# Maxima, denominators and relative positions share one PSUM ring, scores get a fourth bank, and the FFN weights are rounded during attention

## What is computed

```python
q = q / sqrt(hd)
score = einsum('bhqd,bhkd->bhqk', q, k) + einsum('bhqd,qkd->bhqk', q, pe_k)      # pe = rel_emb[clip(k - q, -64, 64) + 64]
attn = softmax(score)
ctx = einsum('bhqk,bhkd->bhqd', attn, v) + einsum('bhqk,qkd->bhqd', attn, pe_v)
x = x + (ctx @ W_out + b_out)                 # on layernorm(x)
h = silu(xq @ wq_gate.T) * (xq @ wq_up.T)     # q: fp4_quant_dequant, blocks of 16
x = x + hq @ wq_down.T                        # on layernorm(x)
```

## Time and profile before

| | |
|---|---|
| three runs | 2486.07, 2490.33 and 2491.36 us, median 2490.33 |
| the profiled execution | 2487.88 us |
| its span, first to last instruction | 2486.2 us |
| mean granted TensorE clock | 0.972 |
| busy: PE, DVE, ACT, POOL | 95%, 77%, 58%, 24% of the span |
| projections and the start of attention | 0 to 173 us |
| attention's iterations | 173 to 2041 us |
| FFN weights | 2044 to 2091 us |
| FFN over 32 tiles | 2091 to 2486 us |

### The profile page before, as it was taken

The page is one execution under the profiler, slowest core; times in us unless marked ns, Lnnn a source line. Parts: engine busy times, 40 slices in busy tenths (PEclk is TensorE's granted clock), DMA queues, the critical chain, the costliest instruction groups (busy, mean ns, idle before and its releaser), DMA issues. The chain is left out here.

```text
span 2486.2 us, 48992 instructions
## 1 busy us (share of the span) xinstructions
PE 2349.4 (95%) x19372; PEld 1168.7 (47%) x19372; DVE 1910.8 (77%) x3509; ACT 1432.6 (58%) x2724; POOL 607.1 (24%) x361
## 2 busy tenths in 40 slices
PE   7899999999999999999999999999999974899997
PEld 3424444444444444444444444444444433666665
DVE  6687777777777777777777777777777707999997
ACT  3416666666666666666666666666666651434432
POOL 5402233222222222222223322222222220111111
PEclk9959999999999999999999999999999995999999
DMA  5733323332334333333323332333332211111110
GB/s 156 200 82 87 88 84 88 88 88 85 109 96 106 95 89 88 89 87 94 89 80 93 88 88 80 92 106 100 95 94 84 74 34 41 41 42 51 42 44 26
DMA packets 275666, 210.43 MB, mean 85 GB/s; under 512 B 17058, under 2 KB 266628, under 8 KB 275332
## 3 DMA queue, kind: packets, MB, share of 16 engines
q1 hardware_dynamic: 274308, 203.37, 30.0%
q0 software_dynamic: 1152, 4.19, 0.6%
HBM read 113.35 MB, written 93.34 MB: 83 GB/s over the span
## 5 line engine op out<-in xcount | busy, mean ns | idle before, releaser
L1049 DVE TENSOR_REDUCE amax<-psA 128x1 f32<-128x512 f32 x2048 | 1312.8, 684 | 407.0 <-PE psA L758 395.4
L1019 ACT ACTIVATE probs<-psS 128x512 f32<-128x512 f32 x1792 | 927.9, 609 | 411.2 <-PE psS L868 411.2
L758 PE MATMUL psA<-keys,queries 96*128 96x512 bf16 x2048 | 771.9, 390 | 1.6 <-DVE amax L1049 1.6
L868 PE MATMUL psS<-queries,keys 102*128 102x512 bf16 (+7 forms) x2176 | 637.5, 344 | 18.9 <-ACT probs L1019 4.1
L784 PE MATMUL psC<-probs,vals 128*32 128x512 f32 (+7 forms) x4352 | 475.0, 524 | 0.1
L719 POOL TENSOR_TENSOR band_probs<-band_probs,side 128x2048 f32<-128x2048 f32 x64 | 288.7, 4533 | 514.2 <-PE psC L880 514.2
L868 PEld LDWEIGHTS psS<-queries,keys 102*128 102x128 bf16 (+1 forms) x2176 | 195.8, 98 | 355.1 <-ACT probs L1019 157.4
L758 PEld LDWEIGHTS psA<-keys,queries 96*128 96x128 bf16 x2048 | 195.7, 97 | 345.5 <-DVE amax L1049 269.1
L1014 ACT ACTIVATE band_probs<-psS 128x512 f32<-128x512 f32 x256 | 153.0, 598 | 152.5 <-PE psS L857 152.3
L998 ACT COPY rel_scores<-psS 128x512 f32<-128x512 f32 x256 | 137.2, 590 | 72.8 <-PE psS L772 72.8
L784 PEld LDWEIGHTS psC<-probs,vals 128*32 128x32 f32 (+1 forms) x4352 | 89.1, 102 | 167.4 <-issue 86.1
(11 more groups left out here) (162 smaller groups left out, 2056.9 us busy)
## 6 DMA issues: line engine op xcount, KB each, us to landing
rel_skew<-rel_scores SPq DMA_DIRECT2D x32, 2048.0 KB, 7.6
rel_near<-rel_skew SPq DMA_DIRECT2D x64, 1024.0 KB, 8.2
keys<-k_ring SPq DMA_DIRECT2D x48, 256.0 KB, 5.8
queries<-q_parts SPq DMA_DIRECT2D x192, 64.0 KB, 2.4
ctx_d<-rden SPq DMA_DIRECT2D x32, 256.0 KB, 2.3
ctx_in<-ctx_d SPq DMA_DIRECT2D x32, 256.0 KB, 2.7
q_parts<-parts SPq DMA_DIRECT2D x16, 384.0 KB, 3.0
k_ring<-parts SPq DMA_DIRECT2D x12, 384.0 KB, 3.3
```

Of the source, the lines that this page charges most:

```text
L758: t.matmul(psA[:, (first + n) % ABANKS, :], qs[0:NR, qb, h, u * P:(u + 1) * P], keys[0:NR, par, h, c0:c0 + NQ], start=True, stop=True).the ...
L868: ins = t.matmul(bank[:, o:o + k], keys[0:nr, par, h, c0:c0 + P], qs[0:nr, qb, h, q0:q0 + k], start=True, stop=True, skip_group_check=True)
L1019: ins = a.activation(probs[:, n % 4, half], src, ACT.Exp)
L1049: v.reduce_max(amax[:, pair, k:k + 1], psA[:, (first + n) % ABANKS, :], AX.X).then_inc(max_taken, 1)
```

## The change

- psM goes. psS gets a fourth bank. P, D and B take slots in the psA ring of three, in TensorE's order (`SLOT`, counted out by `small_slots`); a product waits until the slot three places back was taken, whatever it held. T takes a slot of the psS ring.
- Each P has a slot and a mask of its own, four masks of 256 instead of two of 512. In `ORDER`, P moves ahead of the last M of its step and F ahead of M in step 12.
- The denominators are found by four transposes of `ctxs`, and VectorE reads one column per head. `c.sel` and its two GpSimd instructions go.
- The FFN weights and the bias columns are loaded during iteration 1, and rounded in place by VectorE during attention from iteration 2 on: 16 pieces of 256 or 352 columns, ten operations each, one operation at the start of each of steps 7 to 12. In `ffn_weights`, the transposes of the gate and up rows wait for nothing, VectorE copies out half of them, and W_out's bias products come last.

```diff
-    "SMSSMSMVMP", "SMSSMSMVMP", "SMSSMSMVFMP", "SMSSMSMVMP",
-    "SMSSMSVMF", "SMSSMSVMT", "SMSSMSVM", "SMSSMSVM",
+    "SMSSMSMVPM", "SMSSMSMVPM", "SMSSMSMVFPM", "SMSSMSMVPM",
+    "SMSSMSVFM", "SMSSMSVMT", "SMSSMSVM", "SMSSMSVM",
-SBANKS, ABANKS = 3, 3
+WSTEPS = range(7, 13)
+SBANKS, ABANKS = 4, 3
+def half_at(it, pl, half):
+    return 2 * (first_of(it) + pl) + half + it + 1 + (1 if it < LAST and pl >= place(2 * ASTEPS + 2) else 0)
+def small_slots():
+    slots = {}
+    def add(*key):
+        slots[key] = len(slots)
+    for n in range(ROUND):
+        add("M", 0, n)
+    for n in range(AHEAD):
+        add("M", 1, n)
+    for it in range(LAST + 1):
+        todo = [(it + 1, n) for n in range(AHEAD, ROUND)] if it < LAST else []
+        for step in range(STEPS):
+            if step == ASTEPS and it < LAST - 1:
+                todo.extend((it + 2, n) for n in range(AHEAD))
+            for kind in ORDER[step]:
+                if kind == "M" and todo:
+                    add("M", *todo.pop(0))
+                elif kind == "P":
+                    add("P", it, step - PSTEP)
+                elif kind in "DB" and it:
+                    add(kind, it - 1)
...
-        psM = ctx.enter_context(nc.psum_tensor("psM", [P, NQ], F32))
...
+            def slot_free(*key):
+                pe.wait_ge(small_taken, SLOT[key] + 1)
...
-                pe.wait_ge(max_taken, first + n + 1)
+                slot_free("M", m, n)
...
                 pe.wait_ge(negm_ready, m + 1)
-                t.transpose(psM[0:2 * APAIRS, 0:P], ...
+                pe.wait_ge(unit_done, turn_half(m) + 1)
+                t.transpose(psS[0:2 * APAIRS, turn_half(m) % SBANKS, 0:P], ...
...
                 pe.wait_ge(ctx_copied, it + 2)
+                slot_free("D", it)
                 for u in range(CH):
-                    ins = t.matmul(psM[:, HG * u:HG * u + HG], ctxs[:, u * P:(u + 1) * P], c.sel[:, 0:P:32],
-                                   start=True, stop=True, skip_group_check=True)
+                    ins = t.transpose(small("D", it)[:, u * P:(u + 1) * P], ctxs[:, u * P:(u + 1) * P], c.ident[:])
...
+                if it == 1:
+                    sp.wait_ge(w_set, 4)
+                    fw.load(nc, sp)
...
                 for step in range(STEPS):
+                    if step in WSTEPS and it > 1:
+                        next(weights, None)
...
+                    for kind in ORDER[step]:
+                        if kind == "M":
+                            if todo:
+                                take(*todo.pop(0))
+                            k += 1
+                            if RSTEP < step <= RSTEP + RUNITS and k == 3 and not ends:
+                                rel_maxima(it + 1, step - RSTEP - 1)
+                        elif kind == "P":
+                            mask_positions(step - PSTEP)
+                        elif kind == "D" and not first:
+                            invert(it - 1)
+                        elif kind == "B" and not first:
                             normalise(it - 1)
...
+            def weight_ops():
+                ch = Chain(dve, w_dve)
+                for i, f in [(i, f) for i in range(2) for f in range(FT)] + [(2, f) for f in range(4)]:
...
+                    if ch.n:
+                        ch.hold()
+                    ch.mark(v.tensor_reduce(scale, blk(x), AX.X, ALU.max, apply_absolute_value=True))
+                    yield
...
+                    ch.mark(v.tensor_mul(blk(x), blk(tmp), wide(scale)))
+                    yield
```

In `ffn_weights` after the change:

```diff
+            sp.wait_ge(o_zero, 1)
+            for h in range(HG):
+                sp.dma_start(wo[32 * h:32 * h + HD], w_out.rearrange("(g h d) n -> h d g n", g=NG, h=HG)[h]).then_inc(o_in, 16)
...
+            dve.wait_ge(fw.ends_in, 16 * 2 * HG)
+            oc.mark(v.tensor_scalar(fw.bvc[:], fw.bvc[:], fw.rvc[:, 0:1], None, ALU.add))
...
+            for k in range(KD):
+                dve.wait_ge(w_T, KD + k + 1)
+                v.tensor_copy(wgu[:, k, FFN:FFN + NQ], psW[1][:, k, 0, :]).then_inc(w_copied, 1)
+                v.tensor_copy(wgu[:, k, FFN + NQ:2 * FFN], psW[1][:, k, 1, 0:FFN - NQ]).then_inc(w_copied, 1)
...
             for i in range(2):
                 for k in range(KD):
                     for f in range(FT):
+                        ins = nc.tensor.transpose(psW[i][:, k, f // 4, (f % 4) * P:(f % 4 + 1) * P], fw.raw[i][:, f, k * P:(k + 1) * P],
                                                   c.ident[:])
+            pe.wait_ge(w_copied, 3 * KD)
```

More of the change, by code:

```diff
@@ L73 @@
 BF = 1.5 * 2.0 ** 22
+FT = -(-FFN // P)
+FLAST = FFN - (FT - 1) * P
+GU = FFN // 2
+TINY = 1e-12
 def semaphores(nc, ctx, names):
@@ L835, in half_free @@
                 def half_free(n, half):
-                    pe.wait_ge(unit_done, 2 * (base + place(n, ends)) + half + 1)
+                    pe.wait_ge(unit_done, half_at(it, place(n, ends), half) + 1)
                 def near_half(n, half):
@@ L842, in near_half @@
                     h = 2 * c2 + half
-                    bank = psS[:, (2 * (base + place(n, ends)) + half) % SBANKS, :]
+                    bank = psS[:, half_at(it, place(n, ends), half) % SBANKS, :]
                     if n == 0 and half == 0:
@@ L1009, in iteration @@
                     for half in range(2):
-                        act.wait_ge(unit_ready, 2 * (base + place(n, ends)) + half + 1)
-                        src = psS[:, (2 * (base + place(n, ends)) + half) % SBANKS, :]
+                        j = half_at(it, place(n, ends), half)
+                        act.wait_ge(unit_ready, j + 1)
+                        src = psS[:, j % SBANKS, :]
                         if n < 2 * BAND_STEPS:
@@ L1084, in iteration @@
-                ahead = [] if last and qb >= QB - 2 else [((it + 2) * ROUND, n) for n in range(AHEAD)]
-                def mask_positions(cc):
-                    dve.wait_ge(pos_ready, it * 2 + cc + 1)
-                    v.tensor_tensor(relp[:, cc % 2, :].rearrange("p (x r q) -> p r x q", r=8, q=4),
-                                    psM[:].rearrange("p (r x q) -> p r x q", r=8, q=4),
-                                    c.mask_q[:, None, None, :].broadcast_to([P, 8, APAIRS, 4]), ALU.mult).then_inc(misc_taken, 1)
+                todo = [] if ends else [(it + 1, n) for n in range(AHEAD, ROUND)]
@@ new lines, in iteration, with mask_positions @@
+                ahead = [] if last and qb >= QB - 2 else [(it + 2, n) for n in range(AHEAD)]
+                def mask_positions(k):
+                    ready("P", it, k)
+                    cc, r0 = k // 2, k % 2 * 4
+                    v.tensor_tensor(relp[:, cc, :].rearrange("p (x r q) -> p r x q", r=8, q=4)[:, r0:r0 + 4],
+                                    small("P", it, k)[:, 0:DREL].rearrange("p (r x q) -> p r x q", r=4, q=4),
+                                    c.mask_q[:, None, None, :].broadcast_to([P, 4, APAIRS, 4]), ALU.mult).then_inc(small_taken, 1)
@@ L1119, in _ @@
+            weights = weight_ops()
+            for i in range(2):
+                v.memset(fw.raw[i][FLAST:P, FT - 1, :], 1.0).then_inc(w_set, 1)
+            v.memset(fw.bvc[:], 0.0).then_inc(w_set, 1)
+            v.memset(fw.rvc[:], 0.0).then_inc(w_set, 1)
+            dve.sem_inc(small_taken, ABANKS)
             dve.sem_inc(ctx_out, 16)
-            dve.sem_inc(norm_ready, 1)
             for k in range(RUNITS):
-                rel_maxima(0, 0, k, k)
+                rel_maxima(0, k)
             for n in range(ROUND):
@@ L1136, in _ @@
                 iteration(GRP - 1, qb, last=True)
+            assert next(weights, None) is None
 def pieces(qb, step):
@@ L1564, in ffn_weights @@
-        taps = sb("o_taps_T", [P, NG, HG, 32])
-        raw = [sb(f"w_raw{i}", [P, FT, D] if i < 2 else [P, KD, FFN]) for i in range(3)]
-        wq = [sb(f"w_quant{i}", [P, FT, D] if i < 2 else [P, KD, FFN]) for i in range(3)]
-        tmp = sb("w_tmp", [P, 2, FT * D])
-        bits = sb("w_bits", [P, FT * D])
-        sc = sb("w_scale", [P, 3, 2, FT * D // QBLK])
+        (w_T, w_copied, o_in, o_zero, o_dve, o_taps, o_ready) = semaphores(
+            nc, ctx, "w_T w_copied o_in o_zero o_dve o_taps o_ready")
```

375 lines of the change are left out of this document (171 added, 204 removed).

## The result

The changed kernel takes 2383.67 us (four runs, 2382.3 to 2384.63), the kernel before 2490.11 us beside it: a ratio of 0.9577 (95% interval 0.9563 to 0.9592), 4.2% faster. The forecast was 2397 us, with a range of 2362 to 2442. The profiled execution has a span of 2380.6 us, 105.6 less than before.

The account below looks back on a forecast made before the run. It took TensorE's written order in attention to bound the kernel (TensorE 95% busy). Terms -44.6 - 8 - 4 - 20 + 3 + 13.5 - 31 = -91.1 from 2487.9 gave 2397 us, range 2362 to 2442.

Parts of the forecast that it names:

- Fourth score bank: Attention: score products stop waiting for ScalarE; -44.6 us in steps 5 to 8, -8 in step 3, -4 in last iteration.
- No wait, with 0.15 us to spare: Steps 5 to 8: with four banks S3 and S4 find the copies of R done, 0.15 us to spare.
- Rival C: Steps with R: the wait on ScalarE only moves and they gain nothing; 2442 us, chance 0.08.
- P and F moved: Step 12 and the four P places: fewer changes of TensorE column width, -20 us, bounds -20 and -37.
- D: Denominators by transposes: 0.35 us shorter, 0.37 later start, second M behind waits 0.11; +3 us, bounds -11 to +15.
- P in the ring, masks and weight operations: Steps 8 and 9: VectorE's added work delays the second and third M of step 9, 0.5 us x 27 = +13.5.
- Rival B: Steps 7 to 12: VectorE becomes the bound, weight operations cost their full 56 us, not 13.5; 2440 us, chance 0.13.
- D, an empty ring at six places: Shared ring: TensorE stands until VectorE's answer wherever the kind changes, 0.86 us each, +165; 2545 us, chance 0.05.
- FFN weights: Stage behind attention: 46.7 us becomes 15.8 with weights already rounded, -31 us, bounds -28 to -34.
- 2.87 for the first column operation: FFN weights stage: VectorE's first column operation takes 2.87 us, part of the 7.8 us until its copies are ready.
- 1.2 GHz for the whole stage: FFN weights stage: TensorE's clock stays at 1.2 GHz, w_down's transposes taking 2.6 us and W_out's products 3.6.
- Loads in iteration 1, T, the memsets: Iteration 1's 13 more DMA issues, T in the psS ring and four memsets at the start: no cost.

Follow-up runs that it names:

- ring of four: The changed kernel with the free bank given to the small ring of maxima instead of the scores (psS 3, psA 4): 2416.37 us, 0.9718.
- the rounding beside GpSimd: The changed kernel with the weight operations at the starts of steps 2 to 7, where GpSimd mixes the band, instead of 7 to 12: 2473.11 us, 0.9948.

## Why the prediction was right, point by point

The terms can be read one by one from the traces. A step's length is taken from its first M to the next step's first M; the table has the mean of iterations 1 to 29 in us. The ring of four stands beside the kernel with three score banks, because it has three of them too.

| steps | before | changed | three score banks | ring of four | no rounding |
|---|---|---|---|---|---|
| 1, with D at its end | 4.69 | 4.81 | 4.81 | 4.22 | 4.81 |
| 3 | 2.93 | 2.64 | 2.93 | 2.93 | 2.64 |
| 5 to 7 | 10.54 | 9.41 | 10.54 | 10.55 | 9.41 |
| 8 | 3.93 | 3.47 | 3.82 | 3.83 | 3.46 |
| 9 | 3.56 | 3.75 | 3.49 | 3.46 | 3.56 |
| 10 to 12 | 10.84 | 10.40 | 10.40 | 10.40 | 10.40 |
| the other six | 22.04 | 22.03 | 22.03 | 22.03 | 22.03 |

- **Fourth score bank** (-44.6, -8 and -4: 56.6). Steps 5 to 7 lose nothing any more (-1.13 us), step 8 gains 0.35 by the bank and step 3 its 0.29: 1.77 x 31 = 55 us in the iterations, where 44.6 + 8 were forecast. "No wait, with 0.15 us to spare" held in all four steps; in step 6 one iteration of thirty keeps 0.15 us. Rival C, the wait only moved, is out, but a part did move: 0.26 us an iteration came back as the ring's wait in step 9, which is why taking the bank away costs 53 us and not 60.
- **P and F moved** (-20). 22 by the run. By the steps it is 0.11 each in steps 8 and 9 and 0.44 in steps 10 to 12, 0.66 x 31 = 20. The unseen price, groups of 32 to groups of 64, was taken at 0.13 and measured 0.13: V to P is 1.00 us.
- **D** (+3). Step 1 is 0.12 us longer, x 31 = +4. The sum is right, and partly by luck: D starts 0.99 us behind the first M of the pair where it was 0.53, so 0.46 later and not 0.37; its shorter work is the 0.35 forecast (to the next S it is 0.46 us, where it was 0.81); and the wait of the second M behind D, charged with 0.11, wasn't there.
- **P in the ring, masks and weight operations** (+13.5). The wait is where the forecast put it, at the second and the third M of step 9, and its size was that of the worst iterations. Step 9 has 3.75 us against 3.46 in a ring that doesn't wait: 0.3 x 31 = +9. In every iteration that rounds, the third M waits 0.15 us (0.08 in those that don't). The second waits 0, 0.13 or 0.27 us, by whether step 8's weight operation takes 0.17, 0.28 or 0.42 us; my order of events had 0.33 for every one. Of the 9 us, 6 are the rounding's (3.56 without it), 3 are those of P in a ring of three. Rival B (56 us) is out; so is D, an empty ring at six places: steps 10 to 12 are no longer in a ring of three than in one of four.
- **FFN weights** (-31). Measured 11.2 - 46.7 = -35.5, 4.5 us more. The two failed steps: "2.87 for the first column operation", which was 0.11, so that w_down's transposes start 6.2 us in and not 7.8; and 1.2 GHz for the whole stage, which had priced those and W_out's products at 6.2 us where they took 3.3. In the trace of before the 2.87 us operation (2060.33 to 2063.20) ran beside a GpSimd operation; the rounding beside GpSimd shows that this kind of operation then waits, and the same operation, again the first of its kind in the stage, took 0.11 us with GpSimd idle. That the wait on GpSimd was the cause there is inferred, since I didn't run that stage by itself. The lower bound, -34, was passed for the same two reasons.
- **Loads in iteration 1, T, the memsets** (nothing): the interval between the second and the third start of the negm line, which holds most of iteration 1, is 56.35 us, no longer than those behind it.
- **The whole.** By the starts of the negm line the 31 intervals give -62.9 us. From the last of them to W_out's memset it is 54.4 us, where it was 60.85: -6.4, of which 4 were forecast for the last iteration's waits. The FFN weights give -35.5, the tiles -1.3 (1986.89 to 2380.6, against 2091.20 to 2486.2), the start +0.5. That is the 105.6 us between the spans, and nothing is left over.

The forecast's sum was 14.5 us short (91.1 against 105.6): 4 from the waits in the ring and 4.5 from the stage of the weights, which are mis-sized terms; some 2 each from the fourth bank in the iterations and from the last one; the rest is the tiles and rounding of the terms. Nearly all errors point the same way, so the forecast was on the cautious side and not right by errors that cancel.

## What to carry to other kernels

A busy engine's waits are read off the distance between the starts of the same letters at two places of the schedule, and a bank is worth what the ring that it goes to loses: here 53 us for one ring, 19 for the other. When products of several kinds share a ring, the ring is as slow as the consumer's backlog at the guest's place, so thin out the work just ahead of the guest (two M moved, the rounding out of the way: 14 us by the ratios, 17 by the iterations). And work put into an engine's idle time has to be placed by its neighbours: 54 us of VectorE work cost 0, 6 or 97 us against the kernel without it, depending on which steps held it.

## What the runs showed of the hardware

- VectorE operations with one SBUF tensor and scalars, or with two SBUF tensors, that start while GpSimd's product on SBUF (4.5 us) is running wait for its end: 68 of 69 in the run beside GpSimd. On average they take 1.58 and 1.75 us there where they take 0.17 and 0.42 alone (L1214 and L1232). Reductions and reciprocals stay at 0.39 and 0.22, and takes out of PSUM at 0.62 to 0.69. I had expected it of the first kind only.
- A change of the column group's width costs TensorE 0.10 to 0.13 us in the rows: 0.13 from 32 to the whole array, 0.10 from the whole array to 64, 0.13 from 32 to 64. From 32 to 32 it costs nothing. Order alone was worth 22 us.
- In the stage of the weights TensorE's granted clock was 1.2 GHz while its 24 transposes ran (1975.50 to 1980.86) and 2.4 GHz from their end on, when the products that follow could use it. In the kernel before it rose as well, at the end of a first group of transposes and products (2063.24 to 2069.44), but TensorE then had nothing to do until 2077.69, and by that time the clock was down again. The windows (as above) show it idle at 2.4 GHz, then idle at 1.2:

```profile
2069.40:2072.40 3.00, 0.04 (x1) 0.00 (x0) 2.93 (x3) 0.00 (x0) 0.00 (x0) 1.00 0.00 0
2072.80:2077.60 4.80, 0.00 (x0) 0.00 (x0) 4.70 (x5) 0.00 (x0) 2.77 (x1) 0.50 0.02 3
```
